# First expert layer as three products of split operands, and the last stage's sums and normalisations moved

## The reference

```python
# linear attention, 16 heads of 64
q, k, v = split(x @ W_qkv)
q, k = relu(q @ W_f + b_f), relu(k @ W_f + b_f)
out = (q @ (k.T @ v)) / (q @ k.sum(rows) + 1e-6)      # per head
x = layernorm(x + out @ W_out + b_out)
# mixture of 8 experts, the best 2 of each row
probs = softmax(x @ gate_w.T); p, e = top_k(probs, 2)
h = gelu(x @ w1[e].T + b1[e])                         # 128 -> 512
y = h @ w2[e].T + b2[e]                               # 512 -> 128
x = layernorm(x + sum over the two of p * y)
```

## Time and profile before

| | us |
|---|---|
| median of 3 runs | 473.69 (472.32 to 474.63) |
| profiled execution | 474.31, its span 472.5 |
| PE busy | 437.2 (93%), clock at full speed nearly throughout |
| PEld busy | 343.4 (73%) |
| DVE busy | 300.6 (64%) |
| ACT busy | 273.1 (58%) |
| POOL busy | 162.2 (34%) |

### The profile page before, as it was taken

One profiled execution on the slowest core, in us unless ns is written; L12 is line 12 of the kernel. 1 busy time (PEld: TensorE's weight loads), 2 busy tenths in 40 slices (PEclk: granted clock), 3 DMA queues, 4 the chain that ended last, 5 costly groups with the idle time before them and its releaser, 6 DMA issues.

```text
span 472.5 us, 8134 instructions
## 1 busy us (share of the span) xinstructions
PE 437.2 (93%) x2608; PEld 343.4 (73%) x2608; DVE 300.6 (64%) x896; ACT 273.1 (58%) x531; POOL 162.2 (34%) x164
## 2 busy tenths in 40 slices
PE   4888999999999999999999998799999999999940
PEld 4666776676677677667677674499998999999930
DVE  2654865976976967967967967743563222245784
ACT  2763655665666665665666562278555555555672
POOL 2101101131332233233143133165777545555540
PEclk9999999999999999999999999999999999999995
DMA  8920000000000000000000000598895998799343
GB/s 222 336 70 0 3 0 1 0 19 6 26 23 1 25 23 1 23 25 6 19 24 13 12 25 23 171 318 234 235 276 167 321 286 238 232 337 311 122 134 112
DMA packets 34442, 52.19 MB, mean 110 GB/s; under 512 B 4943, under 2 KB 24788, under 8 KB 34272
## 3 DMA queue, kind: packets, MB, share of 16 engines
q1 hardware_dynamic: 25296, 40.75, 28.4%
q0 software_dynamic: 4544, 8.54, 5.1%
q10 hardware_dynamic: 4560, 2.39, 1.7%
HBM read 39.82 MB, written 12.75 MB: 111 GB/s over the span
## 4 chain that ended last, share of the span: by engine, by line
PE 82%; DVE 6%; DMA 4%; issue 3%; SPq 2%; POOL 2%; ACT 1%; POOLq 0%; DVEq 0%; ACTq 0%
PE psA L639 13%; PE psO L531 11%; PE psG L648 8%; PE psA L434 6%; PE psA L436 6%; PE psA L435 6%; PE psA L510 6%; PE psS L648 5%; PE psG L434 4%; PE psG L551 3%; PE psG L435 3%; PE psG L436 3%; PE psA L578 3%; PE psG L522 3%; DMA x_raw<-x 1%
## 5 line engine op out<-in xcount | busy, mean ns | idle before, releaser
L395 POOL DMA_INDIRECT expert_rows<-rows,pos x64 | 62.5, 977 | 116.7 <-DVE pos L1025 91.1
L419 POOL DMA_INDIRECT expert_results<-q_act,kT x56 | 55.3, 987 | 41.6 <-DVE q_act L1139 30.5
L531 PE MATMUL psO<-qn,mixed 128*128 128x512 f32 x128 | 65.8, 599 | 0.4 <-DVE qn L1056 0.4
L667 ACT ACTIVATE kT<-psA,bf_col 128x512 f32<-128x512 f32 x64 | 44.0, 687 | 37.0 <-PE psA L436 36.7
L667 ACT ACTIVATE q_act<-psA,bf_col 128x512 f32<-128x512 f32 x64 | 43.9, 690 | 26.4 <-PE psA L436 26.3
L1056 DVE TENSOR_TENSOR qn<-q_act,psG 128x512 f32<-128x512 f32 x64 | 43.0, 681 | 5.0 <-PE psG L522 5.0
L820 DVE TENSOR_TENSOR k_lo<-psA,k_hi 128x512 fp32r<-128x512 f32 x64 | 43.7, 686 | 3.5 <-ACT k_hi L667 2.8
L510 PEld LDWEIGHTS psA<-cst,kT 128*128 128x128 f32 x256 | 30.8, 140 | 16.2 <-ACT kT L667 8.3
L794 ACT ACTIVATE q_act<-psA,xT_raw 128x256 f32<-128x256 f32 x84 | 34.6, 471 | 11.8 <-PE psA L639 11.1
L639 PE MATMUL psA<-r_rest,xT_raw 128*128 128x256 f32 x168 | 41.3, 391 | 0.0
L434 PE MATMUL psA<-xT_hi,wk_hi 128*128 128x512 f32 x64 | 41.0, 641 | 0.0
(11 more groups left out here) (180 smaller groups left out, 915.8 us busy)
## 6 DMA issues: line engine op xcount, KB each, us to landing
xT_raw<-w SPq DMA_DIRECT2D x21, 578.0 KB, 4.7
x_raw<-w SPq DMA_DIRECT2D x18, 578.0 KB
kT<-expert_rows SPq DMA_DIRECT2D x28, 132.0 KB, 4.6
x<-expert_results SPq DMA_DIRECT2D x5, 512.0 KB, 6.4
xT_raw<-xT SPq DMA_DIRECT2D x1, 1792.0 KB, 10.4
q_act<-wqkvT SPq DMA_DIRECT2D x3, 512.0 KB, 6.9
rn<-expert_rows SPq DMA_DIRECT2D x11, 132.0 KB, 3.7
out<-x ACTq DMA_DIRECT2D x5, 256.0 KB, 2.3
```

The costliest lines, as they stand in the source:

```text
L395: pool.indirect_dma_start(xs, bass.IndirectOffsetOnAxis(ap=pos[:, j, k:k + 1], axis=0), rows[:, j, k, :], None).then_inc(scattered if o < ...
L419: pool.indirect_dma_start(ys, bass.IndirectOffsetOnAxis(ap=xrow[r][:, c, D:D + 1].bitcast(I32), axis=0), yrow[u][:, c, :], None, bounds_ch ...
L531: mm(psO[:, :], mixed[:, c, :], qn[:, c % 4, :], start=c == 0, stop=c == CH - 1).then_inc(o_pe, 1)
L667: return act.activation(out_, in_, func, **kw)
```

## The change

From block 12 on (`SPLIT`) the first layer is computed as three split products per chunk. For this ACT writes the transposed rows to `xT_hi` in place of `rows_T`, DVE computes `xT_lo` from PSUM, ACT rounds the first-layer weights of the next block (`weight_hi(n + 1)`, 128x512) ahead of the GELUs of block n-1, and DVE takes their rest (`weight_lo(n + 1)`) ahead of the result of block n-2. The halves of `wq_hi` and `wq_lo` serve even and odd blocks.

In the last stage the fetches, sums, chains and normalisations get other passes: one batch's sums at every second pass, the chain of batches 0 to 3 one pass later, those of 4 to 6 together at the end, and only batch 0 is normalised among the blocks. Batches 6 and 7 are fetched into `vo`, so two waits on earlier outputs go.

```diff
-FETCH = {31: 0, 32: 1, 33: 2, 34: 3, 37: 4, 38: 5}
-STAT_AT = {31: 0, 32: 1, 33: 2, 35: 3, 37: 4, 38: 5, 40: 6}
-CHAIN_AT = {36: (0, 4), 39: (4, 6), 40: (6, 7)}
-NORM_AT = {37: 0, 38: 1, 39: 2}
+FETCH = {30: 0, 31: 1, 33: 2, 34: 3, 37: 4, 38: 5}
+STAT_AT = {30: 0, 32: 1, 34: 2, 36: 3, 38: 4, 39: 5, 40: 6}
+CHAIN_AT = {37: ((0, 4),), 40: ((4, 6), (6, 7))}
+NORM_AT = {38: 0}
 PAIRED = 8
+SPLIT = 12
...
-                for space, i in ((x1_space, 0), (x1_space, 1), (x1_space, 2), (x1_space, 3), (qn_space, 0), (qn_space, 1), (x1_space, 0), (x1_space, 1))]
+                for space, i in ((x1_space, 0), (x1_space, 1), (x1_space, 2), (x1_space, 3), (qn_space, 0), (qn_space, 1), (vo, 0), (vo, 1))]
...
                 wait_stored(NEEDS[g])
-                if g >= 6:
-                    sp.wait_ge(f_out[g - 6], 16)
...
             wait_stored(NBLK)
-            sp.wait_ge(f_out[1], 16)
...
                     pe.wait_ge(e_Th, before(n))
+                    if before(n) > SPLIT:
+                        pe.wait_ge(e_Tl, before(n) - SPLIT)
...
                 at = slice(v * BLK, (v + 1) * BLK)
+                if n >= SPLIT:
+                    pe.wait_ge(e_Tl, n - SPLIT + 1)
+                    pe.wait_ge(e_wl, n - SPLIT + 1)
                 for c in range(FC):
+                    if n >= SPLIT:
+                        w = slice(v * F + c * P, v * F + (c + 1) * P)
+                        three(psH[v][:, c, :], wq_hi[:, w], wq_lo[:, w], xT_hi[:, at], xT_lo[:, at]).then_inc(e_up, 1)
+                        continue
...
+            def weight_hi(n):
+                v, u = n % 2, n % SLOTS
+                act.wait_ge(e_w[u], 16 * (n // SLOTS) + 16)
+                if n >= SPLIT + 2:
+                    act.wait_ge(e_up, FC * (n - 1))
+                hi(wq_hi[:, v * F:(v + 1) * F], w_raw[u][:, 0:F]).then_inc(e_wh, 1)
+
...
-                    hi(rows_T[:, v * BLK:(v + 1) * BLK], psX2[bank_of(n)], scale=2.0).then_inc(e_Th, 1)
+                    to = rows_T if n < SPLIT else xT_hi
+                    hi(to[:, v * BLK:(v + 1) * BLK], psX2[bank_of(n)], scale=2.0).then_inc(e_Th, 1)
+                if SPLIT <= n + 1 < NBLK:
+                    weight_hi(n + 1)
                 if n >= 1:
                     gelu(n - 1)
...
-            for g in range(3, B):
+            for g in range(1, B):
                 last_norm(g)
...
+            def weight_lo(n):
+                v, u = n % 2, n % SLOTS
+                dve.wait_ge(e_wh, n - SPLIT + 1)
+                lo(wq_lo[:, v * F:(v + 1) * F], w_raw[u][:, 0:F], wq_hi[:, v * F:(v + 1) * F]).then_inc(e_wl, 1)
+
             last_router = Router(B - 1)
             for n in range(NBLK + 2):
+                if SPLIT <= n < NBLK:
+                    at = slice(n % 2 * BLK, (n % 2 + 1) * BLK)
+                    dve.wait_ge(e_Th, n + 1)
+                    dve.scalar_tensor_tensor(xT_lo[:, at], psX2[bank_of(n)], 2.0, xT_hi[:, at].bitcast(F32), ALU.mult, ALU.subtract).then_inc(e_Tl, 1)
+                if SPLIT <= n + 1 < NBLK:
+                    weight_lo(n + 1)
                 if n >= 2:
                     result(n - 2)
...
-                    last_chain(*CHAIN_AT[n])
+                    for groups in CHAIN_AT[n]:
+                        last_chain(*groups)
```

More of the change, by code:

```diff
@@ L253, in program @@
         e_x, e_w, e_out = ([sem(f"{n}{u}") for u in range(ROW_SLOTS)] for n in ("e_x", "e_w", "e_out"))
-        e_T, e_Th, e_up, e_gelu, e_down, e_y0, e_y1, e_y = (
-            sem(n) for n in ("e_T", "e_Th", "e_up", "e_gelu", "e_down", "e_y0", "e_y1", "e_y"))
+        e_T, e_Th, e_Tl, e_wh, e_wl, e_up, e_gelu, e_down, e_y0, e_y1, e_y = (
+            sem(n) for n in ("e_T", "e_Th", "e_Tl", "e_wh", "e_wl", "e_up", "e_gelu", "e_down", "e_y0", "e_y1", "e_y"))
         in_xr0, in_fold_q, in_fold_v, tab_step = (sem(n) for n in ("in_xr0", "in_fold_q", "in_fold_v", "tab_step"))
```

## The result

| | before | after |
|---|---|---|
| median of 12 runs each | 473.57 (471.49 to 474.96) | 477.95 (472.80 to 480.64) |
| profiled execution | 474.31, span 472.5 | 477.05, span 475.2 |
| mean granted clock | 0.983 | 0.977 |

The ratio is 1.0075, with a 95% interval of 1.0046 to 1.0105: slower, by 0.75%, past the 0.5% within which the prediction speaks of no change, though the lower end of the interval (0.46%) is just inside it. The ratio compares means; one run of the change, 480.64, counts as slow and is left out of it. The forecast was 475.1, no change that a measurement can tell, with slower as the second case. The time came out 2.9 above the forecast, inside the range (470.8 to 479.2) and outside the forecast's own (473 to 477).

What follows compares the result with a forecast made beforehand. TensorE was taken as the bound, with DVE and ACT having room. First layers save 7.35; +3.7, +3.15, +0.65, +0.2 and +1.1 make +1.45: 475.75 profiled, 475.1 as median. Range 470.8 to 479.2, the forecast's own 473 to 477.

Steps and rivals of the forecast that it cites:

- second case: Whole kernel: slower than before by over 0.5%; chance 0.30, against 0.49 for no measurable change.
- load of 17: second layer of 15: Pass 17: GELUs of block 15 wait behind conversion of block 17's late weights; second layer 15 at 371.7, +3.7.
- 21 first layers: Second layer 15 to pass 39: first layers of twelve 0.115 pairs, 0.35 saved each, -7.35 in all.
- load of 31: Before second layer 29: block 31's weights go out behind the moved fetch of batch 0 and land late, +3.15.
- DVE behind it: Behind block 31's wait: low weights, result 28 and sums delay the low rows of 31, +0.65.
- passes with sums, to 36: Passes with sums: DVE's low rows come 0.1 late each time, 0.2 to 0.3 in all.
- from 36 to the last result: Passes 37 to 39: chain of batches 0 to 3 and queued sums on DVE delay the last result, +1.1.
- behind the last result: Kernel end: from last result to the last sums' data it stays 8.75, so 0.
- signs of being wrong: Wrong if PE does not stop in pass 17, plain passes stay over 3.5, or ScalarE's norms hold the end.
- low rows to 3.7; PE wants them at 3.6: Pass with sums: times into the pass at which DVE ends the low rows and PE needs them; 0.1 late.
- is waited away: Passes 13 to 17: four first layers save 1.4 us, all lost since pass 17 still waits for block 17's rows.
- slower rival: First-layer pair: a fixed 0.017 makes it 0.124, the 21 save 5.25, time 477.2; decides from 0.119; chance 0.27.

Runs made afterwards that it cites:

- split products alone: The change with only the split first layer; fetches, sums, chains and normalisations at the passes of before: 477.19, ratio 1.0050 to before.
- early weights, second set: The change with SP issuing the weights of 17 and 18 before its wait for the last scatter, on a slower chip: 492.18, ratio 1.0030 to before.

## Why the prediction was right or wrong

The timelines of PE give the budget by the starts of second layers (block 15: before 367.81, after 370.67; 16: 371.54, 375.84; 28: 416.32, 417.04; 29: 420.06, 422.37; 30: 423.79, 426.77; 36: 446.18, 448.94; last result 455.01, 458.46).

| term | forecast | measured |
|---|---|---|
| load of 17: second layer of 15 | +3.7 | +2.86 |
| low clock behind it, to second layer 16 | not in it | +1.74 |
| 21 first layers | -7.35 | -6.30 |
| load of 31 | +3.15 | +1.90 |
| DVE behind it | +0.65 | +0.97 |
| passes with sums, to 36 | +0.2 | +1.58 |
| from 36 to the last result | +1.1 | +0.69 |
| behind the last result | 0 | -0.75 |
| sum | +1.45 | +2.69 |

That the sum is only 1.24 off is in part luck. Four terms were short, by 4.49 together (pair, low clock, VectorE behind 31, sums), and the other four too long, by 3.25.

**Right.** None of the signs of being wrong that the prediction named came. PE stops in pass 17 for weights and not for rows. The load went out at 364.70 and took 3.81 where I took 4.6 from the earlier trace rows; conversion, GELUs and start followed as put. Block 31 went step by step: fetch 411.71 (forecast 411.55), weights 414.03 (414.2), landed 420.2 (419.7), second layer of 29 at 422.37 (422.15). The term is smaller than 3.15 only because PE came there later by itself; the late time was right. Norms didn't hold the end.

**Pair: the size.** 0.119, not 0.115: of 1.05 the sum is short for that. I had named 0.119 as the point from which the slower case decides. That case came in, but the pair alone doesn't make it: it would be 476.1, and the rest is clock and sums. The Trainium skill (TensorE: Matmul & The Clock Gate, Part 3, The mechanism), cited in the prediction for a pair of 0.214, is contradicted by the 0.119 as by the 0.111. The gap of the same page (Back-to-back issue gap), which it gives for a single matmul, makes 1.31 for twelve, short of the 1.43 measured.

**Clock: a term that was missing.** In "Block 17 ... second layer at 371.7. +3.7" the second layer itself was taken at 1.78. It took 3.33, and the transposes 0.43 for 0.22. The earlier trace rows held no stop of PE in front of a second layer, so nothing in it priced this; but that a stop of about 3 us stands between matmuls was in my own forecast, and I asked only what it delays. The Trainium skill (same page, HAM oscillation, how this bites in real kernels) tells of matmuls that start cold after each wait for a DMA; by it I should have asked. This trace agrees for one stop, clock 0.55 behind that of 2.84, and not for the other: behind that of 1.74 at block 31 it stayed 1.00.

**Sums: the step "low rows to 3.7; PE wants them at 3.6".** Its times were good and its end was missing. In the pass that starts at 443.45 the low rows end at 447.17, which is 3.72 in. But the first layer that reads them starts 0.26 later (447.43), and in others 0.1 more is lost because the result starts 0.2 into the pass (436.03 against 435.83), not 0.05, and once 0.46 goes by between the sums' own steps. So passes with sums take 3.83, 4.19 and 3.85 instead of 3.43. VectorE had room on average (5.91 in 10 us), and yet it set the length of three passes in six. That rests on the timelines; no run took the sums alone out.

**End.** From the last result to the data of the last sums it took 8.00 and not 8.75. The last read-back of results took 2.60 (before 3.19 in the chain) and the last store's landing 2.10 (2.21); that is most of the 0.75, and why they were faster is open.

**From profile to medians.** The profiled pair differs by 2.7, the medians by 4.4, and the ratio of means makes 3.6. The change's runs spread over 7.8 us and those of before over 3.5, though before spread over 7.2 in the 35 runs of the next set. That the stop in pass 17 finds the clock low in some runs for longer than in others would do it (the split products alone had 10 us at half clock in one profile), but I have only one profile of each, so this part is argued, not shown.

**Not forecast as a rule.** I held that what the first layers save ahead of 17 "is waited away". It is more than that: by splitting ahead of 20 one buys nothing and pays the wait for 17's weights. By the ratios `SPLIT = 20` is 1.5 under before and the change 3.6 over it.

## What to carry to other kernels

Before a new early user of a load is added, find the one load that is issued latest behind a barrier, and follow its chain to the engine that bounds the time; start the change behind that load rather than with it. Where PE is made to stand for 2 to 4 us, price the work after the stop at the lower clock as well, as something that can come and needn't. Where a load is sent earlier, look at what lands beside it (the scatter, 4.71 for 2.46). Where two engines hand over in the same tenth of a microsecond, add the handover (0.26 here), and count it once for every pass that has it.

## What the runs showed of the hardware

- A pair of a 128x128 load and 256 columns of f32r goes every 0.119 us at full clock, one with 512 columns every 0.230, and a second-layer pair with 128 f32 columns every 0.111: from the first two I estimate 0.111 for 256 columns and 0.008 for each pair, half of the 0.017 of the slower rival.
- After 2.84 us in which PE stood, the granted clock was at the lower level, and sixteen pairs took 3.33 instead of 1.95; with products run into the gap on another chip 2.05 instead of 3.65. The length of the one stop doesn't decide it: after 2.09 (split products alone) the clock fell to 0.52, after 1.74 and 1.80 it stayed 1.00, and after 2.92 (early weights, second set) it stayed 1.00 as well.
- The same kernel takes 474 on one chip and 490 on two others. On the latter, in the traces of the experiments, GpSimd waits two or three times for 3.0 to 3.7 us for a result between 341 and 373, and the last scatter goes out at 371.2 to 375.4 instead of 360.4. Why those chips are slower is open.
- The same load of 578 KB landed in 3.8, 4.24 and 4.55 us at block 17 on the first chip, in 3.17 and 3.76 on another, and beside two fetches in 6.2 to 6.5.
- The last scatter of rows landed in 2.46 us, and in 4.71 with two loads of 578 KB sent within 3 us ahead of it.
